# Gate and fc products of an MLP by Strassen's seven block products, in a stage of their own before the output projection

## The reference, cut to what matters

```python
h2 = _rms_norm(hs2, norm2_w)                                    # rows of 512
g2 = gelu(h2 @ mlp_gate_w.T + mlp_gate_b, approximate=False)    # 512 -> 1536
f2 = h2 @ mlp_fc_w.T + mlp_fc_b                                 # 512 -> 1536
y  = f2 * g2 @ out_w.T + out_b + hs2                            # 1536 -> 512
x1 = x + y                                                      # read by the FFN half
```

## Time and profile before

| what | value |
|---|---|
| median of three runs (lowest, highest) | 1817.15 us (1816.7, 1817.26) |
| span of the profiled execution, first to last instruction | 1817.1 us |
| mean granted clock of TensorE in it | 0.999 |
| PE busy | 1806.6 us of it |
| DVE, ACT, POOL busy | 998.8, 749.5, 493.0 us |
| first gate product of the MLP half | at 459.6 us |
| first product of the FFN half | at 1275.5 us |

### The profile page before, as it was taken

The page is one execution under the profiler, slowest core; times in us unless marked ns, Lnnn a source line. Parts: engine busy times, 40 slices in busy tenths (PEclk is TensorE's granted clock), DMA queues, the critical chain, the costliest instruction groups (busy, mean ns, idle before and its releaser), DMA issues. The chain is left out here.

```text
span 1817.1 us, 23341 instructions
## 1 busy us (share of the span) xinstructions
PE 1806.6 (99%) x8327; PEld 1472.4 (81%) x8335; DVE 998.8 (55%) x1617; ACT 749.5 (41%) x1144; POOL 493.0 (27%) x462
## 2 busy tenths in 40 slices
PE   9999999999999999999999999999999999999998
PEld 7888888888888888888888888876887787888886
DVE  8766576757742242414142332426985785686555
ACT  7665555556532222222222222233554443544533
POOL 1112212112100000000000000004576887777733
PEclk9999999999999999999999999999999999999999
DMA  5011110012501111110201111165744345444411
GB/s 200 1 47 47 47 46 30 17 47 99 202 1 47 47 47 47 47 47 11 83 1 52 42 47 47 48 211 175 250 129 162 103 154 169 128 151 154 132 43 59
DMA packets 71028, 155.10 MB, mean 85 GB/s; under 512 B 6131, under 2 KB 6387, under 8 KB 70949
## 3 DMA queue, kind: packets, MB, share of 16 engines
q1 hardware_dynamic: 54612, 103.68, 16.8%
q0 software_dynamic: 11776, 41.95, 7.1%
q10 hardware_dynamic: 4560, 8.39, 1.4%
HBM read 120.45 MB, written 33.55 MB: 85 GB/s over the span
## 5 line engine op out<-in xcount | busy, mean ns | idle before, releaser
L309 PE MATMUL bank<-h_parts,gate_w 128*128 128x512 f32 x1536 | 351.5, 390 | 0.6 <-DVE h_parts L624 0.6
L309 PEld LDWEIGHTS bank<-h_parts,gate_w 128*128 128x128 f32 x1536 | 288.1, 188 | 62.3 <-issue 1.4
L1122 DVE SCALAR_TENSOR_TENSOR product_full<-bank,vec_sb,gelu 128x512 f32<-128x512 f32 x96 | 72.0, 750 | 418.5 <-PE bank L903 290.7
L1568 PE MATMUL bank<-operand_parts,int_w 128*128 128x512 f32 x1152 | 282.2, 394 | 0.8 <-DVE u_tiles L2216 0.7
L918 PE MATMUL bank<-product_parts,mlp_out_w 128*128 128x512 f32 x1152 | 280.1, 393 | 0.0
L903 PE MATMUL bank<-h_parts,mlp_fc_w 128*128 128x512 f32 x1152 | 276.8, 389 | 0.0
L903 PE MATMUL bank<-h_parts,mlp_gate_w 128*128 128x512 f32 x1152 | 276.7, 389 | 0.0
L918 PEld LDWEIGHTS bank<-product_parts,mlp_out_w 128*128 128x128 f32 x1152 | 213.2, 188 | 49.5 <-issue 4.6
L903 PEld LDWEIGHTS bank<-h_parts,mlp_gate_w 128*128 128x128 f32 x1152 | 216.2, 188 | 44.9
L903 PEld LDWEIGHTS bank<-h_parts,mlp_fc_w 128*128 128x128 f32 x1152 | 216.2, 188 | 44.9
L1568 PEld LDWEIGHTS bank<-operand_parts,int_w 128*128 128x128 f32 x1152 | 213.0, 188 | 45.5 <-DVE u_tiles L2216 1.6
(11 more groups left out here) (293 smaller groups left out, 2338.1 us busy)
## 6 DMA issues: line engine op xcount, KB each, us to landing
xin<-xT SPq DMA_DIRECT2D x8, 1024.0 KB, 6.8
hs_d<-u SPq DMA_DIRECT2D x8, 1024.0 KB, 5.1
x_columns<-xT SPq DMA_DIRECT2D x8, 1024.0 KB, 5.9
x1T_d<-x_columns SPq DMA_DIRECT2D x8, 1024.0 KB, 5.0
x_tiles<-x_d SPq DMA_DIRECT2D x8, 1024.0 KB, 5.7
out<-u_tiles SPq DMA_DIRECT2D x32, 256.0 KB, 2.8
x_d<-x_rows SPq DMA_DIRECT2D x7, 1024.0 KB, 6.9
raw_w<-int_W SPq DMA_DIRECT2D x7, 1024.0 KB, 8.4
```

The lines of the kernel that those rows point to most:

```text
L309: i = pe.matmul(bank[:], gw[:, w, s, k, m * P:(m + 1) * P], hr[:, q, t, k, :], start=k == 0 and n == 0, stop=k == KT - 1 and n == 2)
L1122: dve.scalar_tensor_tensor(out=pf[:], in0=FB[j % 2][:], scalar=v("mlp_fc_b", j), in1=gg[:], op0=ALU.add, op1=ALU.mult).then_inc(p_full, 1)
L1568: i = pe.matmul(A[m][:], w1[OPER[o]][:, a, k, m * P:(m + 1) * P], op[:, s % 4, c, :], start=s == 0 and n == 0, stop=False)
```

## The change

Gate and fc products are taken out of the block loop. A pair of blocks (tokens t0, t1) is one operand of a 2 x 2 block product: rows are two output tiles of 128 (m = 0, 1), inner blocks the two halves of the 512 channels (kh = 0, 1), columns the two token blocks. Eight block products become seven (the form of Strassen's scheme with four sums of each operand, `FACTORS`). One **group** is one chunk of 256 outputs of one of the two weights (even g: gate, odd g: fc) for one pair of blocks: seven products of 6 matmuls (two 128-channel tiles x three passes). There are 24 **visits** (pair and chunk, `VISITS`), two groups each: 48 groups (`NG`). Two pairs (operands in regions A and B) are at hand at a time, each with 7 split operands (`hop`) of 128x1024; the weights of a chunk are loaded, summed (POOL), split (ACT, DVE) anew for 20 of the 24 visits (`NEW`).

In a group PE's order is: product 1, product 5, product 4 of the group before (`last_product`), 6, 3, 2, 7. Products 1, 6, 7, 4 accumulate into one bank, which is read between them: ACT copies it after 1 (`v1`) and after 6 (`u2`), DVE adds to it after 7 (`c22`), before 4 may be added. ACT copies product 5 (`v5`). DVE makes three sums (`c12`, `c11`, `c22`), ACT three gelus of them for a gate group and one of product 4's bank in the next group, POOL three products gate x fc and DVE the fourth. SP stores the four product tiles of a visit to `p_d`, off chip.

Beside the groups (`beside(g)`), the norm and operands of pair u = 1, 2, 3 are made in six steps, in the groups `LEAD[u]` + 1 to + 6, where `LEAD[u]` + 6 is the pair's first group (LEAD = 0, 18, 24). Pair 0 is made in the last attention block (`early`), both its blocks at once. On ACT `beside(g)` stands behind `u2`; on DVE it stands before the three sums of the group. POOL makes four operand sums for a pair, and POOL's order gets `early(2)` and `early(3)` in the last attention block.

The second stage is the output projection by itself: 96 tiles of 12 matmuls, each tile loaded from `p_d` (DMA issued by ACT), split by ACT and DVE up to four tiles ahead; its weights are loaded and split in groups 44 to 46. `hs2` is loaded a second time. The FFN's preparation steps stand three tiles apart (`HOOK`) over the last three blocks.

```diff
+FACTORS = {1: (A11, B11), 2: (A12, B21), 3: (S4, B22), 4: (A22, T4), 5: (S1, T1), 6: (S2, T2), 7: (S3, T3)}
+HOP_ORDER = (B11, B22, B21, T1, T2, T3, T4)
+NG = 2 * NV
+LEAD = [None] + [FIRST[u] - 6 for u in (1, 2, 3)]
+HOOK = [3 * j + 1 for j in range(FT)]
...
             def body(b, q, nxt, nxt2):
+                if not nxt:
+                    early(-1)
...
                     pool.tensor_tensor(a2[:, m, :], a[:, m, :], a[:, m, :], ALU.mult).then_inc(a_sq, 1)
+                    if not nxt:
+                        early(m)
...
     def sync_program(sp):
         def early_block():
-            sp.wait_ge(att["h_high"], KT * NB)
-            sp.wait_ge(att["h_low"], KT * NB)
-            load(0, 0)
+            sp.wait_ge(att["gates"], KT * (NB - 1))
+            load_pair(0)
...
     def tensor_program(pe):
+        def mean_square(u, n):
+            pe.wait_ge(su_lo, 2 * u + n + 1)
...
+        def last_product(g):
+            pe.wait_ge(c22, g + 1)
+            product(g, 4, X[g % 2], False)
+
+        def group(g):
+            k, i = g % 2, g // 2
+            n = PREP[i]
+            pe.wait_ge(w_lo[k], 2 * n + 1)
...
+            product(g, 1, X[k], True)
+            pe.wait_ge(w_lo[k], 2 * n + 2)
+            if g > 1:
+                pe.wait_ge(c12, g - 1)
+            product(g, 5, Y[k], True)
+            if g:
+                last_product(g - 1)
+            pe.wait_ge(v1, g + 1)
+            product(g, 6, X[k], False)
+            pe.wait_ge(v5, g + 1)
+            product(g, 3, Y[k], False)
+            if g > 1:
+                pe.wait_ge(c11, g - 1)
+            product(g, 2, Z[k], True)
+            pe.wait_ge(u2, g + 1)
+            product(g, 7, X[k], False)
+            for u in (1, 2, 3):
+                if g in (LEAD[u] + 2, LEAD[u] + 3):
+                    mean_square(u, g - LEAD[u] - 2)
...
     def scalar_program(act):
+        def beside(g):
+            for u in (1, 2, 3):
+                step = g - LEAD[u]
+                if step == 1:
+                    squares(u, 0)
+                elif step == 2:
+                    sum_high(u, 0)
+                    squares(u, 1)
+                elif step == 3:
+                    root(u, 0)
+                    sum_high(u, 1)
+                elif step == 4:
+                    root(u, 1)
+                    operand_high(u, B11)
+                elif step == 5:
+                    for o in (B22, B21, T1, T2):
+                        operand_high(u, o)
+                elif step == 6:
+                    for o in (T3, T4):
+                        operand_high(u, o)
...
+            if NG - 4 <= g < NG - 1:
+                out_weights_high(g - NG + 4)
...
+        def group(g):
+            k = g % 2
...
+            copy_of(cp[k][0], X[k], g, 0, v1)
...
+            copy_of(cp[k][1], Y[k], g, 1, v5)
+            if k == 1:
+                gelu_21(g - 1)
+            for what in w_preps(g):
+                weights_high(*what)
+            act.wait_ge(p_ps[6], g + 1)
+            act.wait_ge(c12, max(g - 1, 0))
+            copy_of(cp[k][2], X[k], g, 0, u2)
+            beside(g)
+            if k == 0:
+                for t, added in enumerate((c12, c11, c22)):
+                    act.wait_ge(added, g + 1)
+                    act.activation(gl[t][:], gl[t][:], ACT.Gelu).then_inc(gelu, 1)
...
+    def gpsimd_program(pool):
+        def group(g):
+            for u in (1, 2, 3):
+                if g == LEAD[u] + 4:
+                    operand_sums(u)
+            for what in w_sum_preps(g):
+                weight_sums(*what)
+            if g % 2:
+                multiply(g // 2)
+
+        def early(m):
+            if m == 2:
+                operand_sums(0)
+            elif m == 3:
+                weight_sums(0, 0)
+
+        def run():
+            weight_sums(1, 0)
+            for g in range(NG):
+                group(g)
...
     def vector_program(dve):
+        def beside(g):
+            for u in (1, 2, 3):
+                step = g - LEAD[u]
+                if step == 1:
+                    add_squares(u, 0)
+                elif step == 2:
+                    sum_low(u, 0)
+                    add_squares(u, 1)
+                elif step == 3:
+                    normalise(u, 0)
+                    sum_low(u, 1)
+                elif step == 4:
+                    normalise(u, 1)
+                    operand_low(u, B11)
...
+            if NG - 4 <= g < NG - 1:
+                out_weights_low(g - NG + 4)
...
+        def group(g):
+            k, i = g % 2, g // 2
+            if k == 0 and i:
+                product_21(i - 1)
+            for what in w_preps(g):
+                weights_low(*what)
+            beside(g)
+            for t, (r, copied, bank, n, added) in enumerate(((3, u2, Y, 2, c12), (2, v1, Z, 0, c11), (7, v5, X, 1, c22))):
+                dve.wait_ge(p_ps[r], g + 1)
+                dve.wait_ge(copied, g + 1)
...
+                dve.tensor_tensor((gl, po)[k][t][:], bank[k][:], cp[k][n][:], ALU.add).then_inc(added, 1)
```

## The result

The changed kernel took **1880.69 us** in the median of 4 runs (1880.09 to 1881.81), the kernel before 1816.93 in the same comparison (1815.33 to 1817.26): ratio 1.0353, 95% interval 1.0339 to 1.0368. It is 3.5% slower. The profiled execution has a span of 1878.3 us against 1817.1, so 61.2 us are to be explained; forecast were 36.

What follows compares the result with a forecast made beforehand. PE alone was taken to bound the MLP. On 1817.1 us, - 65.3 + 49.5 + 29.5 + 10 + 3 + 10 = + 36.7 gives 1853.8, stated as 1853; range 1822 to 1880 (the forecast's own 1835 to 1868).

Steps and rivals of the forecast that it cites:

- What is removed: Gate and fc products: 2304 matmuls become 2016, 288 fewer at 0.2267 us, 65.3 us less.
- Pairs 1 to 3: Preparation beside groups: PE waits 14.5 us a pair, 6 more for pair 2; 49.5 us, cheapest 36, dearest 58.
- The 7 us: Pairs' preparation: DVE and POOL alternating on the shared SBUF port would add some 7 us; left out of the sum.
- The last attention block: Pair 0's two blocks made there: 3 us later mean, waits of 13, 8.4 (`v1`) and 5.3 (`u2`); sum 29.5.
- Output weights: Groups 44 to 46: loads and split late, 8.6 us wait and about 1.7 for the next two; 10 us (6.5 to 13).
- Second stage: Output projection: tiles cost nothing, loads keep their places, FFN's last step on DVE delays lows; 3 us (0 to 8).
- Clock: Lower clock after pauses: 1.7 us for six of the dozen pauses over 4 us; 10 us (0 to 20).
- rival (c): Each pause drops the clock for longer: 12 to 14 pauses at 2.5 us, + 33 for + 10; 1877, chance 13%.
- Rival (a): Preparation hidden after all: pairs cost nothing and the clock little, - 19; 1798, chance 10%.
- (b): Shortest chains and a steady clock: sum + 1, with part of the clock + 2 to + 6; 1820, chance 10%.
- (d): Second stage starves: a tile takes 3.2 us by ACT's DMA issues or slow landing, + 46; 1900, chance 4%.
- (e): First stage's products no cheaper, bank changing every six matmuls: 0.24 for 0.2267, 27 us given back; 1880, chance 3%.

Runs made afterwards that it cites:

- c1: Changed kernel without the preparation of pairs 1 to 3 (loads too), all 48 groups multiplying pair 0's operands: 1804.99 us, ratio 0.9926 to the kernel before.
- i1: Changed kernel with the reciprocals of pairs 1 to 3 left out, blocks multiplied by the root instead: 1862.03 us.
- a1: Changed kernel with dummy matmuls, result unused, filling PE's pauses to hold the clock: 1873.81 us.
- e1: Changed kernel with the three output weight loads issued one visit earlier on SP (group 42 for 44): 1874.53 us.
- f1: Changed kernel with the last stage's nine conditioning weight and row loads issued behind output block 5's x load instead of ahead: 1877.06 us.
- g3: Changed kernel, whole computation kept, with pair preparation, attention's end, output weight loads and x load relaid, then five more orders changed: 1823.89 us.
- g4: g3 with two u2 copies ahead of the weight sums' high part and group 1's weight-sum low part ahead of the last scans: 1822.13 us.
- b1: Changed kernel with only VectorE's order changed for pairs 1 to 3 (second sum's low and bank sums before the norm, B11's low later): 1877.13 us.
- d1: Changed kernel with only the last attention block and group 0 reordered on GpSimd, ScalarE and VectorE, group 1 awaiting single gelus: 1883.85 us.

## Why the prediction was wrong, step by step

The direction, the mechanism and the places were right; the size was not: 1853 forecast, 1880.7 measured, 0.7 us outside the range. The step that failed most is the term of the pairs, forecast at 49.5 us and measured at 63.7 with the clock held; next the second stage, 3 forecast and 12.3 measured.

- **What is removed**: -65.3. Right (0.2270 a matmul in c1's row for 0.2267).
- **Pairs 1 to 3**: +49.5 forecast. This is the term that was mis-sized. From the table, with the clock held: 18.4 + 1.4 + 28.4 + 18.2 - 2.7 = **63.7**, outside my dearest, 58. The two large pauses were right, 6.34 for 6.5 and 4.04 for 4.3, and i1 shows their chain. Missing were what stands around them: about 1.5 us in the group of the second squares, 1.2 more than the 3.7 for the summed operands, and in pair 2 the groups at and behind the change of chunk (23 and 25, 2.3 and 2.8 us). Each wait of this kind is a us or two, and I had costed the groups between the large ones at nothing. Part of it is what I left to the upper end, VectorE and GpSimd lengthening each other; how much was not separated. Without the held clock, PE's idle time in groups 2 to 31 was 49.1 us, just the forecast; but 92 slow matmuls there, some 21 us, stood in the place of waits. So that the idle time came out right is luck: the forecast was for full clock, and there the waits are longer. The Trainium skill, SBUF — State Buffer, "SBUF: two separate sides", has it that GpSimd and a VectorE operation with two SBUF inputs take the shared port pair in turns. The 1.70 for 0.72 and 3.44 for 1.23 us above agree, and so does the 0.74 beside sums with a bank. The 7 us that I had worked out for it should have been in the sum.
- **The last attention block**: +29.5 forecast. Group 0 starts 13.3 later (472.93 for 459.61), and groups 0 and 1 take 16.5 over their due: **29.8**. Right in the sum (its terms add up to 29.7, not 29.5); within it `v1` cost 5.18 for 8.4 and `u2` 2.63 for 5.3, but with the clock held they are 6.9 and 5.4 (a1): TensorE's slower products had stood in their place.
- **Output weights**: +10 forecast, 9.9 in groups 45 and 46 (8.2 with the clock held); right, and e1 shows the load as the cause.
- **Second stage**: +3 forecast, waits of **12.3**. The step that said "the hs2 store, x loads and row stores keep their places and have a block of 32.6 us each" failed. The load kept its place in the order of issues, not its distance: it follows the first of the conditioning weights by 11.4 us (1211.17 to 1222.56) where it was 15.3, took 12.7 us for 6.1, and VectorE, which had 8.5 us to spare at it, waited 10.98. f1 shows the weights' part; what the tiles of the intermediate, which share the DMA engines, add to it was not separated. I had looked at the mean rate of the stage (220 of 250 GB/s) and not at who is queued where the rate is at its top.
- **Clock**: +10 forecast, **12.2** by a1 within the first stage. Right in size, and by luck in part: the clock was low behind all the larger pauses (95.6 us in 13 stretches), which is rival (c)'s count, and the slow matmuls add up to its + 33 (some 34 us); but with the clock held more than half of that comes back as waits, which rival (c) did not have. So (c)'s time, 1877, came near the measured one without its mechanism being the whole. The 1.7 us that I multiplied were misread besides: the matmuls of the earlier trace rows do not follow a stretch of almost nothing, since TensorE had worked from 2.29 us on, and the clock fell at 13.30, in their midst. The Trainium skill, TensorE: Matmul & The Clock Gate, "HAM oscillation — how this bites in real kernels", has the drops behind waits as this trace shows them. It counts half of the time at the lower level as lost; here that would be 44 us in the first stage (an estimate from its rule and the 88.7), and a1 gained 12.2 by taking 78.5 of the 88.7 away.
- The sum with the measured sizes, at full clock where a1 gives it: - 65.3 + 63.7 + 29.3 + 8.2 + 12.3 + 12.2 = + 60.4, for 61.2 in the span (29.3 is 29.8 with a1's 16.0 for 16.5). 0.8 us stay open.
- **Rival (a)**, preparation hidden, is refuted by c1 (75.7 us); (b) too, by the 1880.7; (d) is refuted, the tiles do not starve PE in general (four waits); (e) is refuted by c1's row.

Where the gain went, then: the 65 us taken from TensorE are there, and c1 shows the kernel below 1817 as soon as the pairs cost nothing. What eats it is the preparation on the other engines. Relaid, the pairs still cost 9.7 + 0.9 + 12.7 + 10.9 - 2.7 = 31.5 us (g3), the attention's end 26 (group 0 starts 5.2 later than before, and groups 0 and 1 take 21.1 over their due) and the second stage 6: nearly all of 65. (These are of g3's profiled execution, the fastest of its five.) Order was worth 59 us of the 64 lost; the last 5 were still there after g3 and g4, which gained 3 together. That they are load, and not an order that I did not find, is argued from the shared slowing above and not shown.

## What to carry to other kernels

When an algorithm takes work from the bound engine and gives work to the others, cost the places where preparation meets the steady loop, group by group and with the small waits too: a pause in a tight ring of banks is not one number but a tail of smaller ones. Test the idea by leaving the preparation out; that one run says what there is to win before the order is tuned. And a wait removed by reordering is only gained if the engine has idle time up to the next wait: four of the reorderings here (b1, d1, g3, g4) for the most part moved it on.

## What the runs showed of the hardware

- The lower clock level costs less than its share of time where another engine sets the next wait: with it taken away in 78.5 of the first stage's 88.7 us, 12.2 us were gained, where the 119 matmuls no longer slowed would make 27.
- A 1 MB load took 12.7 us instead of 7.8 when issued behind 4 MB of others at 393 GB/s, at nearly the same time (1222.56 and 1222.06).
- GpSimd's 128x256 sum of two SBUF tiles took 0.72 us with VectorE idle, 0.74 beside VectorE's sums with a bank, and 1.70 beside its operations on two SBUF tiles; VectorE's 128x1024 on two SBUF tiles took 1.23 with GpSimd idle and 3.44 beside it.
